# A gated-expert layer behind a long convolution on one core: loop body rotated, set-up reordered

## The chip, the cores and the metric

The kernel runs on one core of one Trainium2 chip. The metric is device time in microseconds (us) of one launch; before the change it is 697.43 us, the median of three runs (694.74 to 697.51).

## The reference, cut to what matters

`x` is 64 sequences x 64 heads x 1024 samples, float32.

```python
# L0, for every head h: a causal convolution over the 1024 samples
mask = (jnp.arange(Lq) < length[:, None])
u_m = u * mask[:, None, :]
kernel = _get_kernel(log_dt, C, log_A_real, A_imag, Lq)   # sum over 64 complex modes of Cs * exp(dtA * l)
y = irfft(rfft(u_m) * rfft(kernel))[..., :Lq] + u_m * D
x = x + y * mask[:, None, :]
# L1, for every (sequence, head) row of 1024
base = x @ W.T
logits = x @ Wr.T + bias_of_language
topw, topi = top_k(logits, 2); weights = softmax(topw)
x = x + base + 2.0 * sum over the two experts of weight * (x @ A_e.T) @ B_e.T
```

## The kernel before

**Pairs.** The work is 32 pairs of heads, numbered i = 0 to 31; a pair has 2 x 64 = 128 rows of 1024 samples. In the code a pair is (b, m) with i = 2b + m, and four heads (two pairs) share one set of generated powers. Every large product is made of three matmuls on float32r halves: high x high, low x high, high x low. ScalarE (ACT) writes the high half (a rounding copy), VectorE (DVE) the low half (the value minus the high half). Names ending in `_hi` and `_lo` are these halves; nearly every one is a hand-off ACT to DVE to TensorE (PE).

**Stages of a pair i.**
- `turn_rows` (PE): eight transposes of the rows of x into the PSUM tile `px`. `split_rows`: ACT copies `px` to `xt` and to `u_hi`, DVE writes `u_lo`.
- `turn_powers` (PE) transposes the generated powers `Z2` into PSUM; `split_ctr` copies them to `c_hi`, `c_lo` and reduces the first 128 samples of the kernel to `k_col`. That column goes to DRAM (`kpad`) and comes back as a Toeplitz tile `toe` (SyncE queue, SP); `split_toe` makes `t_hi`, `t_lo`. `split_obs` makes `zo_hi`, `zo_lo`.
- `control` (PE, 6 matmuls of 448 columns): the input of each block of 128 samples to the modes, into `px` (`v_psum`).
- `scan_states` (DVE, 16 instructions in eight dependent groups of two; ACT swaps real and imaginary halves for it, `copy_states` and three times `swap_odd`): carries the states from block to block. `split_states` makes `s_hi`, `s_lo`.
- `convolve` (PE, 12 matmuls): near part, 6 of 512 columns, from `u` and `t`; far part, 6 of 448 columns, from `s` and `zo`, into `pc`.
- `merge` (DVE) adds it into `xt` where the mask is set; `split_y`: ACT `y_hi`, DVE `y_lo`.
- `project_bank` (PE, 72 matmuls): `y` times the transposed weights in three PSUM banks. The first done (bank 2) holds the router's logits and the experts' 128 inner values. `route` (DVE, 13 small instructions, with one `ratio` from ACT between them) makes `gated`; PE transposes it, `split_gated` halves it, `add_lora` (9 matmuls in all) adds the experts' part. ACT copies the banks to `result` and stores them (`finish`).

**Order.** Each engine has its instructions in an order written by hand; an engine does not pass a waiting instruction. PE's step(b, m), L1132: `convolve(i+1)`, `project_bank(i)` bank 2, `control(i+2)`, `turn_powers(i+3)`, then the other two banks, with the transpose of `gated` and `turn_rows(i+3)` inside the third. DVE's step: `merge(i+1)`, `split_y(i+1)`, `route(i)`, `scan_states(i+2)` with `split_ctr(i+3)`, `split_obs(i+3)`, `split_toe(i+2)` and `split_gated(i)` put between its groups, `split_states(i+2)`, `split_rows(i+3)`. ACT follows the same order. The loop runs 14 times over two steps, and three more steps and a last projection stand behind it.

**Set-up.** The parameters of the modes are computed on DVE in 70 small dependent instructions (`par_step`), among them a polynomial `exact_exp(expo, ...)`. The weights arrive in 11 tiles (`TILE`: A, B, Wr and eight of W), each transposed on PE into a PSUM place, copied to `w_hi` by ACT and to `w_lo` by DVE. The first projection waits (L1042 to L1044 and L1093) until all tiles are done.

Of the kernel before, what the change touches and what calls it, by code (L numbers as in the profile page):

```python
# [13 lines left out]
P = 128  # L14
# [27 lines left out]
def cond_resid_kernel(nc, x, lengths, languages, log_dt, C, log_A_real, A_imag, D, W, Wr, A, B, out):  # L42
    kpad = nc.dram_tensor("kpad", (PAIRS, KPITCH, 2), F32, kind="Internal").ap()
    with ExitStack() as ctx:
# [67 lines left out]


# [38 lines left out]
        xt1_rows = xt[1][:, :, :].rearrange("p c t -> p (c t)")  # L152
        w_rows = [xt1_rows, rows[0][:, :], result[0][:, :], result[1][:, :], result[0][:, :], result[1][:, :],
                  rows[1][:, :], result[1][:, :]]
        a_rows = result[0][:, :]
        b_rows = sb("b_rows", [P, EXPERTS, 8, RANK])
        b_sorted = sb("b_sorted", [P, 8, EXPERTS, RANK])
# [11 lines left out]
        in_pm2 = pm[:, 2, :]  # L169

        def par_psum(k):
# [4 lines left out]
        TILE = [(A_, in_pm, 0), (B_, in_pc, 0), (W_, in_pm, 6), (W_, in_pc, 0), (WR_, in_pm2, 0), (W_, in_pm, 7),  # L176
                (W_, in_pc, 1), (W_, in_pm, 2), (W_, in_pc, 3), (W_, in_pm, 4), (W_, in_pc, 5)]
# [5 lines left out]
        def tile_views(k, wide, narrow):  # L183
            what, place, n = TILE[k]
            if what == B_:
                return place, narrow[:, :].rearrange("e (p o) -> e o p", o=8)
# [32 lines left out]
        sin_ready, z_ready = sem("sin_ready"), sem("z_ready")  # L219
        z_swapped, z2_ready = sem("z_swapped"), sem("z2_ready")  # L220
# [10 lines left out]
        A_STEPS = 25  # L231
        C2_STEPS = 70

        @block.sync
        def _(sp):
# [21 lines left out]
            def load_toe(b, m, first=False):  # L257
                i, s = 2 * b + m, m % 2
                sp.wait_ge(k_stored, 16 * i + 16)
                if not first:  # L260
                    sp.wait_ge(tlo_ready, i - 1)
                sp.dma_start(toe[s][:, :, :], bass.AP(kpad.tensor, i * (2 * KPITCH) + 2, [[2, P], [2, P], [1, 2]])
                             ).then_inc(toe_in[s], 16)

            load_rows(0, 0)
            sp.dma_start(a_rows, A.rearrange("e r d -> (e r) d")).then_inc(a_in, 16)
            sp.dma_start(b_rows[:, :, :, :].rearrange("p e o r -> p e (o r)"),
                         B.rearrange("e (p o) r -> p e (o r)", o=8)).then_inc(b_in, 16)
            sp.dma_start(d_col[:, :], D.rearrange("(h a) -> h a", a=1)).then_inc(d_in, 16)
            for n in (6, 0, 7):  # L270
                load_w(n)
            sp.dma_start(wr_rows[:, :], bass.AP(Wr.tensor, 0, [[P, CH], [LEN, EXPERTS], [1, P]])).then_inc(wr_in, 16)
            sp.wait_ge(px_full, 1)
# [3 lines left out]
            sp.dma_start(len_i[:, :], bass.AP(lengths.tensor, 0, [[0, P], [1, SEQS]])).then_inc(small_in, 16)  # L277
            for h in range(2):
                sp.dma_start(lang_i[h * SEQS:(h + 1) * SEQS, :],
                             languages.rearrange("(b a) -> b a", a=1)).then_inc(small_in, 16)  # L280
            sp.wait_ge(tables, 1)
            sp.dma_start(kpad[:, P:KPITCH, :], zeros[:, :, :]).then_inc(pad_stored, 16)
            sp.wait_ge(pad_stored, 16)
            sp.wait_ge(tables, 3)
            sp.dma_start(bass.AP(kpad.tensor, 2 * P, [[2 * KPITCH, PAIRS], [1, 2]]), k_first[:, :]).then_inc(pad_stored, 16)
            store_kernel(0, 0)
# [3 lines left out]
            load_toe(0, 0, first=True)  # L290
            store_kernel(0, 1)
            load_toe(0, 1, first=True)
            sp.wait_ge(wt_full, w_tile(7) + 1)
            load_w(3)
            sp.wait_ge(wt_full, w_tile(1) + 1)
            load_rows(0, 2)
            sp.wait_ge(wt_full, w_tile(2) + 1)
            load_w(4)
            store_kernel(0, 2)
            load_toe(0, 2)  # L300
            sp.wait_ge(wt_full, w_tile(3) + 1)
            load_w(5)

            def step(b, m, ahead=True):
# [61 lines left out]
        def _(act):  # L366
# [33 lines left out]
            def turn_powers(g, staged, first=False):  # L400

                if not first:
                    act.wait_ge(ct_full, 2 * g)
# [781 lines left out]
```

## Time and profile before

| | |
|---|---|
| runs | 697.51, 697.43, 694.74 us |
| profiled execution, its own time | 695.72 us |
| its span in the profile | 693.9 us |
| PE / DVE / ACT busy | 645.8 / 490.0 / 467.8 us (93% / 71% / 67%) |
| mean granted clock of PE | 0.974 |

What lies around the span is 695.72 - 693.9 = 1.8 us. A row of the timeline gives start, duration, engine, line, operation, output <- inputs, shape; what stands in brackets is how long the engine had been idle and what released it. Two matmuls in a row overlap, so what counts for PE is the distance from start to start.

### The profile page before, as it was taken

Reading aid. Unit: us, or ns where it says so; the run is one execution under the profiler, and the core shown is the slowest. Engines: PE = TensorE matmul, PEld = TensorE weight load, DVE = VectorE, ACT = ScalarE, POOL = GpSimd, SP = SyncE. Lnnn points to the kernel's source line nnn. Section 1 sums busy time; section 2 is a strip of 40 time slices with the busy share of each in tenths; the row PEclk is TensorE's granted clock in tenths of the full one; section 3 lists DMA queues with packets and bytes.
Section 4 is the critical chain, followed back from the end, with each engine's and each line's share of the span. In section 5 each row is a group of like instructions: output and inputs, shape, how many; then the busy total and the mean of one; then the engine's idle time right before and its main releaser. Section 6 shows DMA issues by size and latency. Waiting matters only on the chain.

```text
span 693.9 us, 12598 instructions
## 1 busy us (share of the span) xinstructions
PE 645.8 (93%) x3621; PEld 615.2 (89%) x3621; DVE 490.0 (71%) x1531; ACT 467.8 (67%) x973; POOL 20.4 (3%) x46
## 2 busy tenths in 40 slices
PE   3364999999999999999999999999999999999997
PEld 2353899999999999999999999999999999999997
DVE  8876567777776767777776767777776767777621
ACT  4784577677768677677768677777768677675411
POOL 2000000000000000000000000000000000000000
PEclk9875899999999999999999999999999999999999
DMA  7123023222123233223123233223123223221112
GB/s 241 49 69 89 11 68 70 54 52 68 32 67 68 68 68 68 53 53 68 31 68 68 68 68 68 53 53 68 31 68 68 68 68 68 53 53 39 31 32 60
DMA packets 22869, 43.36 MB, mean 62 GB/s; under 512 B 8104, under 2 KB 13512, under 8 KB 22856
## 3 DMA queue, kind: packets, MB, share of 16 engines
q1 hardware_dynamic: 17576, 26.42, 17.1%
q10 hardware_dynamic: 5280, 16.78, 9.5%
q14 instruction: 7, 0.06, 0.1%
q8 instruction: 6, 0.10, 0.1%
HBM read 26.35 MB, written 16.84 MB: 62 GB/s over the span
## 4 chain that ended last, share of the span: by engine, by line
DVE 36%; ACT 25%; issue 18%; PE 13%; ACTq 6%; DMA 2%; DVEq 1%; SPq 0%
DVE state L783 17%; PE pmg L1104 9%; ACTq L470 5%; ACT result L488 4%; ACT u_hi L416 4%; ACT turn L379 3%; ACT L393 3%; DVE y_lo L830 3%; ACT swapped L439 2%; ACT Z L405 2%; DVE Z L770 2%; ACT xt L413 2%; DVE c_lo L764 2%; ACT z_swap L398 2%; PE pc L1029 2%
## 5 line engine op out<-in xcount | busy, mean ns | idle before, releaser
L1104 PE MATMUL pmg<-w_hi,y_hi 128*128 128x388 f32 (+1 forms) x768 | 268.7, 350 | 1.7 <-ACT result L488 0.2
L1104 PE MATMUL pmg<-w_hi,y_lo 128*128 128x388 f32 (+1 forms) x768 | 260.1, 339 | 0.0
L1104 PE MATMUL pmg<-w_lo,y_hi 128*128 128x388 f32 (+1 forms) x768 | 259.8, 338 | 0.0
L1104 PEld LDWEIGHTS pmg<-w_hi,y_hi 128*128 128x128 f32 x768 | 144.3, 188 | 7.5 <-ACT result L488 6.5
L1104 PEld LDWEIGHTS pmg<-w_hi,y_lo 128*128 128x128 f32 x768 | 144.6, 188 | 0.2
L1104 PEld LDWEIGHTS pmg<-w_lo,y_hi 128*128 128x128 f32 x768 | 144.2, 188 | 0.0
L439 ACT ACTIVATE swapped<-state 64x128 f32<-64x128 f32 x192 | 59.3, 309 | 67.1 <-DVE state L783 65.7
L783 DVE SCALAR_TENSOR_TENSOR state<-swapped,scan_tab,state 128x192 f32<-128x192 f32 (+1 forms) x240 | 73.8, 349 | 12.1 <-ACT swapped L439 0.2
L812 DVE TENSOR_TENSOR s_lo<-state,s_hi 128x896 fp32r<-128x896 f32 x32 | 35.0, 1093 | 31.5 <-ACT s_hi L461 31.5
L744 DVE TENSOR_TENSOR u_lo<-xt,u_hi 128x1024 fp32r<-128x1024 f32 x32 | 39.2, 1225 | 24.8 <-ACT u_hi L416 24.8
L461 ACT ACTIVATE s_hi<-state 128x896 fp32r<-128x896 f32 x32 | 30.5, 953 | 35.0 <-DVE state L783 35.0
L783 DVE SCALAR_TENSOR_TENSOR state<-state,scan_tab 128x64 f32<-128x64 f32 x180 | 50.6, 323 | 0.0
L770 DVE SCALAR_TENSOR_TENSOR Z<-z_swap,gen_tab,Z 128x128 f32<-128x128 f32 x56 | 16.0, 347 | 38.8 <-ACT Z L405 38.8
L824 DVE COPY_PREDICATED xt<-valid,pc 128x512 f32<-128x512 int32 x64 | 42.9, 724 | 0.0
L488 ACT ACTIVATE result<-pmg 128x388 f32<-128x388 f32 (+1 forms) x96 | 37.0, 458 | 8.1 <-PE pmg L1079 7.9
L466 ACT ACTIVATE y_hi<-xt 128x1024 fp32r<-128x1024 f32 x32 | 33.5, 1048 | 13.2 <-DVE xt L824 13.2
L830 DVE TENSOR_TENSOR y_lo<-xt,y_hi 128x1024 fp32r<-128x1024 f32 x32 | 39.0, 1220 | 4.0 <-ACT y_hi L466 3.9
L379 ACT ACTIVATE turn<-pos,phase,gen_tab 128x128 f32<-128x128 f32 x56 | 23.1, 484 | 22.6 <-issue 22.6
L1022 PE MATMUL px<-ident,rows 128*128 128x128 f32 x256 | 35.8, 286 | 0.0
L398 ACT ACTIVATE z_swap<-Z 64x512 f32<-64x512 f32 x32 | 20.2, 630 | 19.5 <-issue 19.0
L1022 PEld LDWEIGHTS px<-ident,rows 128*128 128x128 f32 x256 | 32.1, 149 | 1.2
L413 ACT ACTIVATE xt<-px 128x1024 f32<-128x1024 f32 x31 | 31.3, 1010 | 0.7 <-PE px L1022 0.7
(195 smaller groups left out, 1068.1 us busy)
## 6 DMA issues: line engine op xcount, KB each, us to landing
rows<-in_x SPq DMA_DIRECT2D x64, 256.0 KB, 5.1
out<-result ACTq DMA_DIRECT2D x62, 256.0 KB, 3.0
toe<-kpad SPq DMA_DIRECT2D x32, 128.0 KB, 4.5
result<-in_L_cond_W SPq DMA_DIRECT2D x5, 512.0 KB, 7.2
rows<-in_L_cond_W SPq DMA_DIRECT2D x2, 512.0 KB, 7.8
result<-in_L_cond_A SPq DMA_DIRECT2D x1, 512.0 KB, 5.8
b_rows<-in_L_cond_B SPq DMA_DIRECT2D x1, 512.0 KB, 7.0
xt<-in_L_cond_W SPq DMA_DIRECT2D x1, 512.0 KB, 8.8
```

Source lines behind the costliest of these rows:

```text
L379: ins = nc.scalar.activation(turn[:, h, :], pos[:, :], ACT.Identity, bias=phase[:, 0:1], scale=gen_scalar(TURNS, g, h, staged))
L413: nc.scalar.activation(xt[s][:, :, :], px[:, :, :], ACT.Copy).then_inc(xt_ready, 1)
L439: ins = nc.scalar.activation(swapped[out_half, :, chunks, :], source[in_half, :, chunks, :], ACT.Copy)
L470: act.dma_start(bass.AP(out.tensor, (2 * i + h) * LEN + c0, [[HEADS * LEN, SEQS], [1, c1 - c0]]), result[s][h * SEQS:(h + 1) * SEQS, c0:c1 ...
L488: nc.scalar.activation(result[s][:, c0:c1], pm[:, n, 0:c1 - c0], ACT.Copy).then_inc(pm_free, 1)
L744: vec.tensor_tensor(u_lo[s][:, :, :], xt[s][:, :, :], u_hi[s][:, :, :].bitcast(F32), ALU.subtract).then_inc(ulo_ready, 1)
L783: ins = vec.scalar_tensor_tensor(out=state[:, h, chunks, :], in0=source[:, h, at, :], scalar=scan_scalar(name, m if staged else i, h, staged),
L812: vec.tensor_tensor(s_lo[:, :, :, :], state[:, :, :, :], s_hi[:, :, :, :].bitcast(F32), ALU.subtract).then_inc(slo_ready, 1)
L824: ins = vec.copy_predicated(xt[s][:, :, h * SEQS:(h + 1) * SEQS], valid[:, :, :], pc[:, h, :, :])
L830: vec.tensor_tensor(y_lo[s][:, :, :], xt[s][:, :, :], y_hi[s][:, :, :].bitcast(F32), ALU.subtract).then_inc(ylo_ready, 1)
L1022: ins = nc.tensor.transpose(px[:, c, :], rows[s][:, c * P:(c + 1) * P], ident[:, :])
L1104: ins = nc.tensor.matmul(pm[:, n, 0:c1 - c0], y[s][:, c, :], w[:, c, c0:c1], start=(c == 0 and y is y_hi and w is w_hi), stop=(c == CH - 1 ...
```

## The change

On every engine the step is put in another order. PE: projection of pair i in banks 2 and 0, the transpose of `gated(i)`, `control(i+2)`, `convolve(i+1)`, `add_lora` for two banks, the third bank with `turn_rows(i+3)`. `turn_powers(i+2)` stands at the step's head. So everything is made one pair nearer to its use. DVE: `split_ctr(i+2)`, `split_obs(i+2)`, `route(i)`, `split_rows(i+2)`, `split_toe(i+1)`, `split_gated(i)`, `merge(i+1)`, `split_y(i+1)`, and the scan of pair i+2 with nothing between its groups.

```diff
-            def step(b, m, rows_left=True, ahead=True, kernels=True):
-                convolve(b, m + 1)
-                pe.wait_ge(yhi_ready, 2 * b + m + 1)
-                pe.wait_ge(ylo_ready, 2 * b + m + 1)
-                project_bank(b, m, 0)
+            def step(b, m, rows_left=True, ahead=True):
+                if rows_left:
+                    turn_powers(b, m + 2)
+                wait_y(b, m)
+                project(b, m, 0)
+                project(b, m, 1)
+                turn_gates(b, m, 2 * b + m + 3 if rows_left else PAIRS)
                 if rows_left:
                     control(b, m + 2)
+                convolve(b, m + 1)
+                add_loras(b, m)
+                project(b, m, 2, 0, 7)
                 if ahead:
-                    turn_powers(b, m + 3)
-                project_bank(b, m, 1)
-                project_bank(b, m, 2, ahead)
-
-            with pe.Fori(0, LOOPS) as b:
+                    turn_rows(b, m + 3)
+                project(b, m, 2, 7, 8)
+                add_lora(BANK_ORDER[2])
+
+            with pe.Fori(1, LOOPS) as b:
...
                 for m in range(2):
                     step(b, m)
```

ACT's new step:

```diff
+            def step(b, m, rows_left=True, kernels=True):
+                if rows_left:
+                    split_ctr(b, m + 2)
+                    split_obs(b, m + 2)
+                evacuate(b, m - 1, 2)
+                if rows_left:
+                    split_rows(b, m + 2)
+                ratios(b, m)
+                split_toe(b, m + 1)
                 if kernels and m == 0:
                     act.wait_ge(gen_staged, b + 1)
                     turns_of(None, True)
                 if kernels and m == 1:
                     swap_powers(b + 2)
...
+                store(b, m - 1)
+                split_gated(b, m)
...
                 if kernels and m == 0:
                     magnitudes(None, True)
+                    waves(b + 2)
                 if kernels and m == 1:
...
+                    turn_powers(b + 2, True)
+                for j in range(2):
+                    evacuate(b, m, j)
+                split_y(b, m + 1)
                 if rows_left:
                     copy_states(b, m + 2)
...
+                    for n in range(3):
+                        swap_odd(b, m + 2, n)
+                    if kernels and m == 0:
+                        nc.scalar.activation(warm[:, :], phase[:, 0:1], ACT.Exp)
                     split_states(b, m + 2)
```

The loop runs 13 times (pairs 2 to 27); pairs 0 and 1 are written out ahead of it. `project` is `project_bank` cut into ranges of its eight input chunks; `turn_gates` and `add_loras` are pieces of it.

The set-up:

```diff
-        TILE = [(A_, in_pm, 0), (B_, in_pc, 0), (W_, in_pm, 6), (W_, in_pc, 0), (WR_, in_pm2, 0), (W_, in_pm, 7),
-                (W_, in_pc, 1), (W_, in_pm, 2), (W_, in_pc, 3), (W_, in_pm, 4), (W_, in_pc, 5)]
+        TILE = [(A_, in_pm, 0), (W_, in_pc, 6), (W_, in_pm, 7), (WR_, in_pm2, 0), (W_, in_pm, 0), (W_, in_pc, 1),
+                (W_, in_pm, 2), (W_, in_pc, 3), (W_, in_px, 4), (B_, in_pc, 0), (W_, in_px, 5)]
...
+            def kernel_row(j):
+
+                if j:
+                    pe.wait_ge(k_ready, j)
+                for h in range(2):
+                    ins = nc.tensor.matmul(row_psum[:, j, :], pick[:, h, :], Z2[:, 2 * j + h, :], start=h == 0,
+                                           stop=h == 1, skip_group_check=True)
+                ins.then_inc(row_full, 1)
...
+            def sort_b():
+                act.wait_ge(b_in, 32)
+                nc.scalar.activation(b_sorted[:, :, :, :].rearrange("p o e r -> p e o r"), b_rows[:, :, :, :], ACT.Copy
+                                     ).then_inc(b_ready, 1)
...
+            project(0, 0, 0, 0, 3)
             turn_weight(6)
+            project(0, 0, 0, 3, 6)
+            turn_weight(7)
+            pe.wait_ge(v_copied, 2)
+            pe.wait_ge(scan, SCAN + 1)
+            turn_weight(8)
+            project(0, 0, 0, 6, 8)
+            pe.wait_ge(wlo_ready, w_tile(3) + 1)
+            project(0, 0, 1, 0, 4)
+            turn_weight(9)
+            project(0, 0, 1, 4, 8)
+            turn_weight(10)
+            pe.wait_ge(wlo_ready, 10)
+            convolve(0, 1)
+            turn_gates(0, 0, 2)
```

The first projection starts as soon as the four tiles of bank 2 are split (A, W 6, W 7, Wr). The polynomial for `expo` becomes one ACT exponential (56 parameter steps for 70). The powers of the first four heads are finished in two halves. The first two kernels go to DRAM as rows (`kernel_row`, a matmul with a picking matrix) in place of columns. B is sorted by ACT where GpSimd did it, and loaded in two halves. The loads on SP's queue are reordered to the new order of use; W 0 has a buffer of its own.

On PE, in the loop, the step around the transpose of `gated` (`pc` is the convolution's tile, `px` the control's and the rows', `pmg` the projection's). Before:

```order
L1029 MATMUL pc<-s_lo,zo_hi 128x448
L1029 MATMUL pc<-s_hi,zo_lo 128x448
...
L1104 MATMUL pmg<-w_hi,y_hi 128x384
...
L1029 MATMUL px<-u_hi,c_hi 128x448
L1029 MATMUL px<-u_lo,c_hi 128x448
```

and now:

```order
L1220 MATMUL pmg<-w_hi,y_lo 128x388
L1220 MATMUL pmg<-w_lo,y_hi 128x388
L1229 REGISTER_ALU
L1230 MATMUL pmg<-ident,gated 128x128
L1159 MATMUL px<-u_hi,c_hi 128x448
L1159 MATMUL px<-u_lo,c_hi 128x448
L1159 MATMUL px<-u_hi,c_lo 128x448
L1159 MATMUL px<-u_hi,c_hi 128x448
L1159 MATMUL px<-u_lo,c_hi 128x448
L1159 MATMUL px<-u_hi,c_lo 128x448
L1165 REGISTER_ALU
L1159 MATMUL pc<-u_hi,t_hi 128x512
```

The control of pair i+2 stood 24 projection matmuls behind the convolution of pair i+1; now it stands directly in front of it, and the transpose of `gated(i)` in front of both.

On DVE, in the loop, the rows of the scan and what follows. Before:

```order
L783 SCALAR_TENSOR_TENSOR state<-swapped,scan_tab,state 128x3x64 x2
L762 REGISTER_ALU
L763 TENSOR_REDUCE k_col<-pmg 128x2
L764 TENSOR_TENSOR c_lo<-pmg,c_hi 128x256
L755 SCALAR_TENSOR_TENSOR zo_lo<-Z,sigma,zo_hi 128x256
L796 REGISTER_ALU
L783 SCALAR_TENSOR_TENSOR state<-state,scan_tab 128x64 x2
```

and now, from the scan's last group to the halves that PE waits for:

```order
L885 SCALAR_TENSOR_TENSOR state<-swapped,scan_tab,state 128x3x64 x2
L914 TENSOR_TENSOR s_lo<-state,s_hi 128x896
L855 REGISTER_ALU
L857 TENSOR_REDUCE k_col<-pmg 128x2
L858 TENSOR_TENSOR c_lo<-pmg,c_hi 128x256
L848 SCALAR_TENSOR_TENSOR zo_lo<-Z,sigma,zo_hi 128x256
...
L940 TENSOR_TENSOR logits<-pmg,bias 128x8
...
L964 TENSOR_TENSOR gated<-pmg,gates 128x128
L837 TENSOR_TENSOR u_lo<-xt,u_hi 128x1024
```

`c_lo` and `zo_lo` stood between groups of the scan and now stand behind it; `route` stood in front of the scan and now stands behind it; `u_lo`, which came last, still does, but is now of pair i+2 and not of pair i+3.

## Rows read from the trace of the kernel before

**Rows 1.** The page: busy us, share of the span and instructions of each engine.
```profile
PE 645.8 (93%) x3621; PEld 615.2 (89%) x3621; DVE 490.0 (71%) x1531; ACT 467.8 (67%) x973; POOL 20.4 (3%) x46
```
**Rows 2.** Busy time by stretch: us, PE, PEld, DVE, ACT, POOL, clock, DMA share, GB/s.
```profile
0.00:77.36 77.36, 38.08 (x167) 32.85 (x168) 55.63 (x173) 47.01 (x88) 4.29 (x19) 0.78 0.36 103
77.36:693.90 616.54, 607.74 (x3455) 582.37 (x3453) 434.36 (x1358) 420.76 (x886) 16.07 (x27) 1.00 0.26 57
```
**Rows 3.** Timeline of PE: first matmuls of convolutions 1, 2, 13, 14, 30, and a control.
```profile
74.71 0.47 PE L1029 MATMUL pc<-u_hi,t_hi 128*128 128x512 f32 x1 [0.76 <-DVE w_lo L737]
...
93.88 0.39 PE L1029 MATMUL pc<-u_hi,t_hi 128*128 128x512 f32 x1
...
308.58 0.39 PE L1029 MATMUL pc<-u_hi,t_hi 128*128 128x512 f32 x1
...
315.39 0.36 PE L1029 MATMUL px<-u_hi,c_hi 128*128 128x448 f32 x1
...
316.61 0.38 PE L1073 MATMUL pmg<-ident,Z 128*128 128x128 f32 x2
...
327.72 0.39 PE L1029 MATMUL pc<-u_hi,t_hi 128*128 128x512 f32 x1
...
639.98 0.39 PE L1029 MATMUL pc<-u_hi,t_hi 128*128 128x512 f32 x1
```
**Rows 4.** Timeline of DVE behind the convolution of pair 30.
```profile
642.85 0.15 DVE L816 COPY held<-lang_f 128x1 f32<-128x1 f32 x1 [1.69 <-PE pc L1029]
...
649.90 0.74 DVE L783 SCALAR_TENSOR_TENSOR state<-state,scan_tab,px 128x192 f32<-128x192 f32 x2 [0.57 <-ACT swapped L439]
...
656.69 1.09 DVE L812 TENSOR_TENSOR s_lo<-state,s_hi 128x896 fp32r<-128x896 f32 x1 [1.02 <-ACT s_hi L461]
```
**Rows 5.** Timeline of ACT in the same stretch.
```profile
644.30 1.06 ACT L466 ACTIVATE y_hi<-xt 128x1024 fp32r<-128x1024 f32 x1 [3.43 <-DVE xt L824]
...
648.20 0.60 ACT L447 ACTIVATE state<-px 128x512 f32<-128x512 f32 x1 [0.45 <-PE px L1029]
```
**Rows 6.** Timeline of DVE in the loop: route, c_lo and zo_lo, u_lo, powers.
```profile
316.74 0.16 DVE L838 TENSOR_TENSOR logits<-pmg,bias 128x8 f32<-128x8 f32 x1
...
317.61 0.15 DVE L848 TENSOR_SCALAR half_sum<-ratio 128x1 f32<-128x1 f32 x1
...
319.01 0.74 DVE L783 SCALAR_TENSOR_TENSOR state<-state,scan_tab,px 128x192 f32<-128x192 f32 x2
...
320.45 0.28 DVE L763 TENSOR_REDUCE k_col<-pmg 128x2 f32<-128x128 f32 x1
...
321.38 0.47 DVE L783 SCALAR_TENSOR_TENSOR state<-state,scan_tab 128x64 f32<-128x64 f32 x2
...
328.44 1.23 DVE L744 TENSOR_TENSOR u_lo<-xt,u_hi 128x1024 fp32r<-128x1024 f32 x1 [0.81 <-ACT u_hi L416]
330.49 0.69 DVE L635 TENSOR_TENSOR Z<-angle,mag 128x512 f32<-128x512 f32 x1 [0.81 <-ACT angle L393]
```
**Rows 7.** Timeline of ACT in the loop: s_hi, xt, and the table load.
```profile
325.56 0.95 ACT L461 ACTIVATE s_hi<-state 128x896 fp32r<-128x896 f32 x1 [1.10 <-DVE state L783]
326.42 1.01 ACT L413 ACTIVATE xt<-px 128x1024 f32<-128x1024 f32 x1
...
336.21 1.28 ACT L569 ACT_TABLE_LOAD   x1
337.50 0.20 ACT L569 ACTIVATE warm<-phase 128x1 f32<-128x1 f32 x1
```
**Rows 8.** Timeline of PE in the set-up: first control, and transposes behind idle time.
```profile
23.47 0.71 PE L1029 MATMUL px<-u_hi,c_hi 128*128 128x448 f32 x1 [1.22 <-DVE c_lo L764]
...
64.56 1.94 PE L1002 MATMUL pmg<-ident,result 128*128 128x128 f32 x8 [5.34 <-DVE w_lo L737]
```
**Rows 9.** Timeline of DVE in the set-up: first scan, last low half of a weight tile.
```profile
27.79 0.74 DVE L783 SCALAR_TENSOR_TENSOR state<-state,tab,px 128x192 f32<-128x192 f32 x2 [1.43 <-ACT swapped L439]
...
73.34 1.22 DVE L737 TENSOR_TENSOR w_lo<-pc,w_hi 128x1024 fp32r<-128x1024 f32 x1 [4.10 <-ACT w_hi L370]
```

More of the change, by code:

```diff
@@ L314, in _ @@
                     step(b, m)
-            step(LOOPS, 0)
+            step(LOOPS, 0, rows_left=False)
         @block.gpsimd
@@ new lines, in _ @@
+            split_states(0, 0, first=True)
+            weight(2)
+            split_rows(0, 1, first=True)
+            weight(3)
+            split_obs(0, 1, first=True)
+            split_y(0, 0)
+            weight(4)
+            copy_states(0, 1)
+            weight(5)
+            swap_odd(0, 1, 0)
+            turns_of(1, False)
+            weight(6)
+            swap_odd(0, 1, 1)
+            weight(7)
+            swap_odd(0, 1, 2)
+            waves(1)
+            weight(8)
+            split_toe(0, 1, toe_rows_back)
@@ new lines, in _ @@
+            split_obs(0, 3)
+            evacuate(0, 0, 2)
+            split_rows(0, 3)
+            ratios(0, 1)
+            split_toe(0, 2)
+            act.wait_ge(gen_staged, 1)
+            turns_of(None, True)
+            magnitudes(None, True)
+            store(0, 0)
+            split_gated(0, 1)
+            waves(2)
+            evacuate(0, 1, 0)
+            evacuate(0, 1, 1)
+            split_y(0, 2)
+            copy_states(0, 3)
+            swap_odd(0, 3, 0)
+            swap_powers(2)
@@ L935, in _ @@
-            next(scanning)
+            split_y(0, 1)
+            split_rows(0, 2)
             split_ctr(0, 2)
-            next(scanning)
-            split_toe(0, 1)
-            split_states(0, 1)
             split_obs(0, 2)
-            for k in range(7, WTILES):
-                low_weight(k)
-            split_rows(0, 2)
-            def step(b, m, rows_left=True, ahead=True, kernels=True):
+            dve.wait_ge(scan_staged, 1)
+            for _ in scan_states(0, 2):
+                pass
@@ new lines, in _, with step @@
+            split_states(0, 2)
+            split_ctr(0, 3)
+            split_obs(0, 3)
+            route(0, 1)
+            split_rows(0, 3)
+            split_toe(0, 2)
+            angles(2)
+            split_gated(0, 1)
+            merge(0, 2)
+            powers(2)
+            split_y(0, 2)
+            for _ in scan_states(0, 3):
+                pass
+            rotate_powers(2, True)
+            split_states(0, 3)
+            def step(b, m, rows_left=True, kernels=True):
+                if rows_left:
+                    split_ctr(b, m + 2)
+                    split_obs(b, m + 2)
@@ L1158, in _ @@
[L1158 to L1162 removed]
+            step(LOOPS, 0)
+            step(LOOPS, 1, ahead=False)
+            step(LOOPS + 1, 0, rows_left=False, ahead=False)
+            wait_y(LOOPS + 1, 1)
+            project(LOOPS + 1, 1, 0)
+            project(LOOPS + 1, 1, 1)
+            turn_gates(LOOPS + 1, 1, PAIRS)
```

574 lines of the change are left out of this document (314 added, 260 removed).

## Prediction

> **What bounds the kernel now.** I read the page first: PE is busy 93% of the span, DVE 71%, ACT 67% [rows 1]. Split by stretch it falls into two kernels [rows 2]. Up to 77.4 us, where the first projection starts, PE is busy 38.1 of 77.4 us at a granted clock of 0.78: a set-up bound by chains. From there PE is busy 607.7 of 616.5 us at clock 1.00: PE is the bound, and DVE (434.4) and ACT (420.8) have some 180 us of room by their sums. The timeline of PE gives the beat. From the convolution of pair 2 (93.88) to that of pair 30 (639.98) there are 28 intervals: 546.1 / 28 = 19.50 us a pair [rows 3]. Between those of pairs 13 and 14, where PE never waits, it is 327.72 - 308.58 = 19.14 us; that is PE's own work for a pair. So the loop can give 0.36 us x 28 = 10 us at most, and the set-up more. What the shares do not tell is how long the chain through DVE and ACT is from one convolution to the next, and the change lengthens just that.
>
> **The loop: the chain that the new order makes.** Let N be the start of a convolution's first matmul, pair i. I follow DVE's new program from there, with durations of the old trace.
>
> 1. `held` starts at N + 2.87 (639.98 to 642.85), `y_hi` at N + 4.32 (644.30) [rows 3 to 5]. In the new order `copy_states(i+1)` stands directly behind `y_hi`: 1.06 less the 0.09 by which two ACT instructions overlap, then 1.70 to the scan's first instruction (648.20 to 649.90) [rows 4, 5]. The scan starts at N + 6.99.
> 2. From there to `s_lo` the row has 6.79 us (649.90 to 656.69) [rows 4], with `t_lo` and `gt_lo` (0.54 together) standing in holes where DVE waits for ACT's swaps. Without them the holes remain: I take 6.64. `s_lo` starts at N + 13.63. In every other step (m = 0) ACT loads the exponential's table and runs `warm` between the last swap and `s_hi`: 1.29 + 0.20 [rows 7], of which 1.06 lie beside the scan's last group. Behind such a step `s_lo` starts 0.43 later, at N + 14.06.
> 3. `s_lo` 1.00 start to start, then `k_col`, `c_lo`, `zo_lo` 0.93 (320.45 to 321.38) [rows 6]: N + 15.56, or N + 15.99. In steps m = 1 `powers` comes in between, 0.69 less 0.09 of overlap [rows 6]: 16.59.
> 4. `route`: 0.87 to `half_sum`, which needs ACT's `ratio`. `s_hi` starts 0.98 before `s_lo` (its 0.95 and a hand-off), and on ACT follow `s_hi` 0.86, `c_hi` 0.28, `zo_hi` 0.40, a bank's copy 0.40, `xt` 0.90, `u_hi` 0.95 (start to start, as s_hi and xt in [rows 7]) and `ratio` 0.29: N + 16.73 in steps m = 0. So `half_sum` starts at N + 16.76 (m = 0) and at 16.59 + 0.87 = N + 17.46 (m = 1).
> 5. From `half_sum` to the next instruction 1.40 (317.61 to 319.01), then `u_lo` 1.23 [rows 6]: done at N + 19.39 or N + 20.09. The control of pair i+2 can start some 0.12 later (a first matmul behind `c_lo` in [rows 8] came 0.15 after it) and takes 316.61 - 315.39 = 1.22 [rows 3]. Then the next convolution starts: **N + 20.72 or N + 21.42**, mean 21.07.
>
> PE by itself would be there at N + 19.14. In the old order the control's half `u_lo` was made a pair ahead, the far part alone waited for `s_lo`, and `c_lo`, `zo_lo` lay in the holes of the scan. Now `s_lo`, `c_lo`, `route` and `u_lo` stand one behind the other, and control and the whole convolution (3.8 us of PE) stand behind their end. The price is 21.07 - 19.50 = 1.57 us a pair. Nothing hides it: PE's other 15 us of the pair are issued ahead of the wait and lie beside the chain already. ACT has no wait of its own in it: `gt_hi`, the waves and the two bank copies end just before `y_hi` is due (by my count with 0.1 us of room in steps m = 0, so it can only add). SP's loads of rows and Toeplitz tiles are issued a whole pair ahead of use, as before, and cost nothing.
>
> **The set-up.** 14 parameter steps go, and the rest is better placed: parameters 1.7 us earlier. With the first powers in two halves the first control starts at about 20.1 for 23.47 [rows 8]. ACT then has weight tiles and the second half to do, so the first scan starts at 26.2 for 27.79 [rows 9]; convolution 0 ends at 37.3, `y_lo` of pair 0 at 41.2. The first projection starts at 42.6 for 77.4, cut up by the transposes of the last tiles, which still come at the rate of ACT and DVE: the last low half is done at 62.6 for 73.34 + 1.22 = 74.6 [rows 9]. The third bank ends at 69.2; `y_hi`, `xt`, `u_hi` of the next two pairs stand in line on ACT (3 x 1.0 us), control 2 starts at 73.6, the projection of pair 1 at 75.0, its two banks are done at 84.7. Then comes the chain of steps 2 to 5 for the first time: scan at 76.6, `route(1)` ends at 87.9, `t_lo(2)` at 89.4. Convolution 2 starts at **89.6** for 93.88 [rows 3], 4.3 us earlier, and PE has by then done two banks of pair 1 besides, 8.5 us of matmuls that the old order did later. So the set-up alone is worth 4.3 + 8.5 = 12.8 us. The transposes in it run at half rate behind idle time (1.94 us for eight at 64.56, [rows 8]); where PE now stays busy they are shorter, which is in the figures. The row form of the first two kernels (four 128-column matmuls, two small copies), ACT's sort of B (about 1.0 us) and the small extra loads lie beside other work: if the sort were bare, it would cost 1 us once.
>
> **The sum.** Convolution 2 at 89.6. Step 2 is irregular: ACT has the swap and the scaling of the next heads' powers between its three swaps of the state (2.5 us, less 0.2), so convolution 3 starts 23.0 later, 112.6. Then 13 steps of 21.42 and 12 of 20.72 (pairs 3 to 27): 527.1, to 639.7. Two steps without kernels, 20.72 each: 681.2. The last convolution comes 17.35 later, there is no control in front of it: 698.5. Behind it on PE three banks, two banks, and the rest, 22.6, last copy 0.5, last store 3.7: span 725.4. With 1.8 around it 727.2 us against 695.7 of the profiled execution: 31.5 us or 4.5% slower. The profiled execution lies 1.7 below the median of 697.4; I forecast **728 us**.
>
> Between bounds: the chain cannot be under PE's 19.14 a pair, and the sum of its parts with each of about twelve hand-offs 0.05 us shorter or longer gives 20.5 to 21.7 a pair, 16 us down and 18 up over 28 pairs.
>
> **A rule against the trace.** The table load in the chain lasts 1.28 us, and `warm` starts 0.01 us behind it [rows 7]. The Trainium skill (ScalarE: Activation LUTs, What ACT_TABLE_LOAD costs) gives a switch of tables as about 2.66 us, with a drain behind the load. By that figure every other step would be 1.38 us longer, 13 x 1.38 = 18 us in all, an estimate of 745 us. The row shows no such drain, so the sum goes by the row.
>
> **The rivals.**
> - *The chain is hidden* (10%). If waits overlap better than I count and the beat stays PE's own, the gain of the set-up stands: 695.7 - 12.8 = 682.9, and with 0.2 to 0.3 us a pair of the old waits gone too some 676; say 682. For it: DVE is busy only 14.3 of 19.5 us a pair. Against it: an in-order queue adds its waits, and the old trace shows them (1.02 before `s_lo`, 0.81 before `u_lo`, [rows 4, 6]). The point from which it decides is a beat under 21.07 - 31.5 / 28 = 19.95 us.
> - *A draw* (5%): a beat of 19.8 to 20.1, 692 to 700 us.
> - *ACT late too* (7%). The 0.1 us of room in steps m = 0 is gone as soon as ACT's two stores or register work cost more than I count. Each us there comes back on `y_hi` and delays everything: 13 us a microsecond; 742 us.
> - *The table's drain* (3%), 745 us, as above.
> - *The clock falls in the waits* (2%). PE will stand idle 1.6 to 2.3 us in each pair. In the old trace matmuls behind 5.3 us of idle ran at half rate [rows 8], at clock 1.2 GHz for 2.4; gaps of this length after full rate it does not show. If control and convolution ran at 1.2 GHz, 3.8 us more would stand in the chain each time: over 100 us. The Trainium skill (TensorE: Matmul & The Clock Gate, HAM oscillation) warns of loops in which every round's wait brings the slow clock back.
> - *The change doesn't do what it says*: if the first projection had to wait for the last tile all the same, the set-up would give only 2 or 3 us and the whole came to 738. It is in the range.
>
> My forecast has the remaining 73%.
>
> **How the numbers follow.** Range: 20 us below 728 (a beat of 20.35, a little beyond the lower bound of the hand-offs, because I may have counted waits twice) and 14 above (a beat of 21.55, or ACT late by a microsecond): 708 to 742. That leaves out the hidden chain, the draw and the far tail, some 2 in 10. Faster by over 0.5% (about what a measurement can tell from no change): the 10% of the hidden chain and a part of the draw, 0.11. Within 0.5%: 0.04. Slower: 0.85.
>
> **What would show it.** In the new profile: convolutions 20.7 and 21.4 us apart by turns; PE busy some 88 to 90% of the span at clock 1.00 in the loop; a wait of PE at the control's matmul for DVE's `u_lo`, or at the transpose of `gated`, of 1.6 to 2.3 us a pair and some 50 us in all; `ratio` holding DVE 0.3 us in steps m = 0; convolution 2 at about 90 us. Wrong would be: a beat of 19.2 with PE's waits near nothing; PE released by ACT's bank copies or by SP's loads; or a first projection not before 60 us.

## The result, and the profile after

The changed kernel takes 735.30 us (median of 4 runs, 733.52 to 736.74) against 696.36 us of the kernel before in the same session (4 runs, 694.74 to 697.51): a ratio of 1.056, 95% interval 1.052 to 1.060. The forecast was 728 us, in a range of 708 to 742. The profiled execution took 734.07 us, its span 732.3.

Page of the changed kernel, busy time of the engines (the same lines of before are [rows 1]):

```profile
PE 658.6 (90%) x3629; PEld 616.8 (84%) x3629; DVE 495.0 (68%) x1518; ACT 465.5 (64%) x980; POOL 19.1 (3%) x38
```

Its work by stretches (columns: stretch, length, busy time and instructions of PE, weight loads, DVE, ACT and POOL, PE's granted clock, DMA share, GB/s):

```profile
0.00:42.00 42.00, 24.27 (x100) 19.69 (x101) 34.26 (x125) 27.49 (x55) 1.07 (x9) 0.80 0.54 161
42.00:96.00 54.00, 42.66 (x237) 39.33 (x235) 34.92 (x94) 34.98 (x70) 0.40 (x2) 0.91 0.23 54
96.00:679.00 583.00, 543.93 (x3033) 512.04 (x3032) 403.50 (x1223) 386.69 (x821) 17.65 (x27) 0.99 0.24 54
679.00:732.30 53.30, 47.71 (x264) 45.76 (x263) 22.36 (x78) 16.36 (x35) 0.00 (x0) 0.99 0.18 43
```

Before, PE had waited 8.8 us in all the 616.5 behind the set-up [rows 2]. Now it is idle 39 of 583 us in the third stretch, at a clock of 0.99. The first projection begins at 42.5 us for 77.4; the forecast was 42.6.

PE's waits in the loop, 115 to 690 us (waiting instruction, its releaser, us in total, times, longest):

```profile
PE px L1152 <- DVE state L885: 11.4, 27, 0.5
PE px L1159 <- DVE u_lo L837: 10.1, 13, 0.8
PE px L1159 <- issue: 8.2, 14, 0.6
PE pmg L1230 <- DVE gated L964: 5.6, 13, 0.4
```

PE ahead of the convolutions 14 and 15 (start, us, engine, line, operation, tiles; idle time before it):

```profile
349.68 0.32 PE L1230 MATMUL pmg<-ident,gated 128*128 128x128 f32 x1 [0.44 <-DVE gated L964]
350.78 0.44 PE L1159 MATMUL px<-u_hi,c_hi 128*128 128x448 f32 x1 [0.78 <-DVE u_lo L837]
...
352.09 0.40 PE L1159 MATMUL pc<-u_hi,t_hi 128*128 128x512 f32 x1
...
371.38 0.44 PE L1159 MATMUL px<-u_hi,c_hi 128*128 128x448 f32 x1 [0.58 <-issue]
...
372.66 0.39 PE L1159 MATMUL pc<-u_hi,t_hi 128*128 128x512 f32 x1
```

And DVE between these two convolutions:

```profile
354.98 0.15 DVE L918 COPY held<-lang_f 128x1 f32<-128x1 f32 x1 [3.76 <-PE pc L1159]
...
359.06 0.74 DVE L885 SCALAR_TENSOR_TENSOR state<-state,scan_tab,px 128x192 f32<-128x192 f32 x2 [0.32 <-ACT swapped L479]
...
365.61 1.09 DVE L914 TENSOR_TENSOR s_lo<-state,s_hi 128x896 fp32r<-128x896 f32 x1 [1.02 <-ACT s_hi L501]
...
368.67 0.15 DVE L950 TENSOR_SCALAR half_sum<-ratio 128x1 f32<-128x1 f32 x1 [0.17 <-ACT ratio L510]
...
370.06 1.22 DVE L837 TENSOR_TENSOR u_lo<-xt,u_hi 128x1024 fp32r<-128x1024 f32 x1
```

N is, as in the forecast, the start of a convolution's first matmul, here 352.09. This is the chain of the forecast. `u_lo` ends at 371.28, the control's first matmul starts 0.10 later ("issue" is that wait, whose releaser the record lacks), and the convolution stands behind it. In the steps between convolutions 3 and 28 the intervals are 20.57 us (steps m = 0, to an odd convolution) and 21.42 us (steps m = 1, to an even one) by turns, mean 525.5 / 25 = 21.02 us (before: 19.50).

The waits are smaller than the forecast's sign for them, which was 1.6 to 2.3 us a pair at the control or the transpose of `gated`, some 50 us in all. They are 0.44 + 0.78 = 1.22 us in steps m = 1 and 0.58 in steps m = 0, 23.9 us in all; another 11.4 us stand earlier in the step, at the transposes of the rows (L1152), until the scan has read its input out of `px`.

One place was not foreseen. In the loop's first step PE stands at the transposes of the next heads' powers, which now head the step:

```profile
108.37 0.69 PE L1201 MATMUL pmg<-ident,Z 128*128 128x128 f32 x2 [4.40 <-DVE Z L864]
108.71 0.67 PE L1220 MATMUL pmg<-w_hi,y_hi 128*128 128x384 f32 x1
109.18 0.52 PE L1220 MATMUL pmg<-w_hi,y_lo 128*128 128x384 f32 x1
...
113.26 0.34 PE L1220 MATMUL pmg<-w_lo,y_hi 128*128 128x384 f32 x1
```

DVE rotates these powers only behind the scan of pair 3. PE waits 4.4 us, and then multiplies at the lower clock: 15 matmuls start 0.32 us apart for 0.18, until 113, which is 2.1 us. Behind that it waits for nothing up to the convolution. From convolution 2 (91.06) to 3 (120.61) it takes 29.55 us; the forecast had 23.0. The wait and the slow matmuls together, 4.4 + 2.1 us, are as much as the 6.5 between them.

### The profile page after: what moved, and what is told of

It reads as the page before. It is cut to its first block, busy times and chain, and to the rows that moved or that the text cites. A ratio compares the mean times of both kernels' runs of the same rounds, so it can differ in the third digit from the quotient of the medians.

```text
span 732.3 us, 12371 instructions
## 1 busy us (share of the span) xinstructions
PE 658.6 (90%) x3629; PEld 616.8 (84%) x3629; DVE 495.0 (68%) x1518; ACT 465.5 (64%) x980; POOL 19.1 (3%) x38
## 4 chain that ended last, share of the span: by engine, by line
PE 44%; DVE 24%; ACT 16%; issue 14%; ACTq 0%; DVEq 0%; DMA 0%; SPq 0%
PE pmg L1220 22%; PE pc L1159 12%; ACT swapped L479 7%; DVE state L885 6%; PE px L1159 6%; DVE xt L926 5%; DVE u_lo L837 3%; ACT state L487 3%; PE px L1152 2%; ACT s_hi L501 2%; ACT L668 2%; PE pmg L1207 1%; DVE held L918 1%; DVE zo_lo L848 1%; DVE c_lo L858 1%
## 5 line engine op out<-in xcount | busy, mean ns | idle before, releaser
L524 ACT ACTIVATE result<-pmg 128x388 f32<-128x388 f32 (+1 forms) x96 | 43.4, 453 | 100.7 <-PE pmg L1207 100.2
L918 DVE COPY held<-lang_f 128x1 f32<-128x1 f32 x96 | 14.8, 154 | 101.1 <-PE pc L1159 98.9
L932 DVE TENSOR_TENSOR y_lo<-xt,y_hi 128x1024 fp32r<-128x1024 f32 x32 | 39.2, 1225 | 24.0 <-ACT y_hi L506 22.5
L1159 PE MATMUL px<-u_hi,c_hi 128*128 128x448 f32 x64 | 26.3, 410 | 23.7 <-DVE u_lo L837 10.1
L1152 PE MATMUL px<-ident,rows 128*128 128x128 f32 x256 | 35.9, 285 | 11.4 <-DVE state L885 11.4
L1152 PEld LDWEIGHTS px<-ident,rows 128*128 128x128 f32 x256 | 28.8, 145 | 20.2 <-DVE state L885 19.2
L1159 PEld LDWEIGHTS px<-u_hi,c_hi 128*128 128x128 f32 x64 | 12.2, 191 | 31.0 <-issue 30.5
L837 DVE TENSOR_TENSOR u_lo<-xt,u_hi 128x1024 fp32r<-128x1024 f32 x31 | 37.7, 1215 | 0.7 <-ACT u_hi L456 0.7
L456 ACT ACTIVATE u_hi<-px 128x1024 fp32r<-128x1024 f32 x31 | 32.0, 1031 | 0.0
```

What stands on the lines that cost most here:

```text
L524: nc.scalar.activation(result[s][:, c0:c1], pm[:, n, 0:c1 - c0], ACT.Copy).then_inc(pm_free, 1)
L837: vec.tensor_tensor(u_lo[s][:, :, :], source[:, :, :], u_hi[s][:, :, :].bitcast(F32), ALU.subtract).then_inc(ulo_ready, 1)
L932: vec.tensor_tensor(y_lo[s][:, :, :], xt[s][:, :, :], y_hi[s][:, :, :].bitcast(F32), ALU.subtract).then_inc(ylo_ready, 1)
L1152: ins = nc.tensor.transpose(px[:, c, :], rows[s][:, c * P:(c + 1) * P], ident[:, :])
L1159: ins = nc.tensor.matmul(out, l, r, start=first and n == 0, stop=last and n == 2, skip_group_check=True)
```

## Experiments

Unless said otherwise each is the changed kernel with one edit. Ratios are to the kernel before on the same chip. A beat is the interval between the first matmuls of two convolutions in a row; the longer one is that of steps m = 1, the shorter one that of steps m = 0. The runs are numbered in the order in which they were made.

**1. More PE work: does PE or the chain set the beat?**

```diff
+                if j == 1 and c0 == 0:
+                    for _ in range(6):
+                        nc.tensor.matmul(pm[:, n, 0:o1 - o0], y_hi[s][:, 0, :], w_hi[:, 0, o0:o1], start=True,
+                                         stop=False, skip_group_check=True)
```

> The changed kernel with six more matmuls of 388 columns a pair (repeats of the first one, each overwriting the last) ahead of bank 0, 6 x 0.177 = 1.06 us of PE work in front of the place where PE waits. If the chain through DVE sets the beat (my theory), the wait takes it up: in its trace PE waits 1.2 us in steps m = 1 and 0.6 us in steps m = 0 there, so 0.0 and 0.5 us a pair remain, some 5 to 9 us in all: 741 to 744. If PE sets the beat (rival), 31 x 1.06 = 33 us more: 768.

740.84 us, 1.0636 (1.0619 to 1.0654). Some 33 us of matmuls cost 5.5. The longer beat stays (21.46 for 21.42), the shorter one grows by 0.27 (20.84), since 1.06 us are more than the 0.58 that PE waited there, and it now waits there no more. In the changed kernel PE's work lies beside the chain; it is not the bound.

**2. More DVE work in the chain.** A second subtraction of half the size, 0.54 us start to start, in front of `s_lo`:

```diff
+                vec.tensor_tensor(spare[:, :, :], state[:, 0, :, :], s_hi[:, 0, :, :].bitcast(F32), ALU.subtract)
```

> The changed kernel with one more DVE subtraction of 448 elements a pair into an unused tile, directly in front of s_lo; 0.5 to 0.6 us. If the chain sets the beat, nothing absorbs it: 30 x 0.55 = 16 us more, 751 to 753. If DVE's idle time (32% of the span) is room (rival), no change: 735.

765.45 us, 1.0999 (1.0981 to 1.1018): 30 us more, twice what the chain explains. Where the convolutions keep their rate, the beats are 22.09 and 20.87, together 0.97 more than before the edit, about the 0.54 twice, less the 0.17 of `ratio`'s wait, now covered. Over 13 rounds that is 13 us. The rest came out only with run 6: in 11 steps matmuls of the convolution last up to 0.63 us in place of 0.39, and such a pair of steps is 1.5 to 1.6 us longer. In some of them the control is slow already:

```profile
273.25 0.59 PE L1161 MATMUL px<-u_hi,c_hi 128*128 128x448 f32 x1 [0.78 <-DVE u_lo L838]
```

**3. The control behind the convolution and the two `add_lora`.**

```diff
-                if rows_left:
-                    control(b, m + 2)
                 convolve(b, m + 1)
                 add_loras(b, m)
+                if rows_left:
+                    control(b, m + 2)
```

> The changed kernel's steady step with control(i+2) behind convolve(i+1) and its two banks' add_lora, all other orders as they are. Chain theory: the convolution then waits for t_lo, which ends 0.3 us behind u_lo, and not for u_lo and the control's 1.22 us; the beat falls by 0.9 us, 28 x 0.9 = 25 us: 710, beats of 19.7 and 20.5. Rival (the control's place is harmless, the time sits in the late s_lo or in route alone): 730 to 735.

715.11 us, 1.0270 (1.0253 to 1.0287): 20 us less, where I had expected 25. The beats are 20.70 and 19.85. The convolution does not wait for `u_lo` any more but for `t_lo`, which stands right behind it on DVE (1.27 and 0.48 us by turns). So the gain is smaller than with the whole chain gone: `route` and `u_lo`, which stand in front of `t_lo` on DVE, still hold the convolution.

**4. The transposes of the powers behind the first bank, in every step.**

```diff
-                if rows_left:
-                    turn_powers(b, m + 2)
                 wait_y(b, m)
                 project(b, m, 0)
+                if rows_left:
+                    turn_powers(b, m + 2)
```

> The changed kernel's steady step with turn_powers(i+2) behind the first bank and not in front of it. The trace of the changed kernel has one wait of 4.40 us of PE at turn_powers in step 2, for the powers that DVE rotates behind the scan; this wait stood in none of my terms. If it is what my sum of the start lacked, it goes and the first steps are 4 to 8 us shorter, once: 728 to 731, steady beat as it is. Rival: the late powers hold the step anyway through c_lo: 735.

747.20 us, 1.0737 (1.0719 to 1.0755), 12 us more where I had expected less. The first step did shrink (24.0 us for 29.55), but the loop's beats became 21.58 and 21.58. ACT shows why:

```profile
409.84 0.95 ACT L501 ACTIVATE s_hi<-state 128x896 fp32r<-128x896 f32 x1 [1.02 <-DVE state L885]
411.68 0.39 ACT L475 ACTIVATE c_hi<-pmg 128x256 fp32r<-128x256 f32 x1 [0.89 <-PE pmg L1201]
```

`c_hi` reads what these transposes write; they come 0.9 us late for it, and `xt`, `u_hi`, `ratio` stand behind it in the queue. At the step's head they are early in the loop and late only once.

**5. The kernel before, with the control alone moved in front of the convolution.**

```diff
             def step(b, m, rows_left=True, ahead=True, kernels=True):
+                if rows_left:
+                    control(b, m + 2)
                 convolve(b, m + 1)
...
                 project_bank(b, m, 0)
-                if rows_left:
-                    control(b, m + 2)
```

> The kernel BEFORE, with one edit in the loop's steps: the control of pair i+2 stands in front of the convolution of pair i+1, the place it has in the changed kernel; what feeds it stays where it was, so its low half u_lo is made a pair ahead. My theory (the price is the chain c_lo, route, u_lo that the new order puts in front of the control, not the control's place): c_lo is there some 4 us before the control was issued in the old order, but only about when the convolution starts, so PE waits a little at most; beat 19.5 to 19.8 a pair, 696 to 704 us. Rival (the place alone, control and its copies in the chain, costs its own 1.2 us each pair): 28 x 1.2 = 34 us, about 730.

774.91 us, 1.1129 (1.1092 to 1.1166): far outside both expectations. My reading of the old order was wrong. In this run PE's control waits for `u_lo`:

```profile
409.24 1.23 DVE L744 TENSOR_TENSOR u_lo<-xt,u_hi 128x1024 fp32r<-128x1024 f32 x1 [0.80 <-ACT u_hi L416]
```

```profile
410.56 0.44 PE L1029 MATMUL px<-u_hi,c_hi 128*128 128x448 f32 x1 [1.93 <-issue]
```

`u_lo` was not made "a pair ahead". In the kernel before it is the last work of DVE's preceding step: for pair 15 it ends at 329.67 us (328.44 + 1.23, [rows 6]), 1.95 behind the start of convolution 14. The control came only at 334.91, behind that convolution and a bank:

```profile
334.91 0.36 PE L1029 MATMUL px<-u_hi,c_hi 128*128 128x448 f32 x1
```

These 5.2 us were the cover, and moving the control in front of the convolution takes them away: the beats at full rate are 21.4 to 21.8. In 13 of the loop's steps the convolution ran at half rate besides. So the control's place is no harmless part of the change; alone it costs more (79 us) than with DVE's program turned to suit it (39 us).

**6. The table load and `warm` behind `s_hi`.**

```diff
-                    if kernels and m == 0:
-                        nc.scalar.activation(warm[:, :], phase[:, 0:1], ACT.Exp)
                     split_states(b, m + 2)
+                    if kernels and m == 0:
+                        nc.scalar.activation(warm[:, :], phase[:, 0:1], ACT.Exp)
```

> The changed kernel with the loop's table load and warm (once in two steps) behind split_states in place of in front of it. My theory: s_hi no longer waits for the load, s_lo of steps m = 1 starts 0.43 us earlier, but the load then stands between s_hi and c_hi, so that c_hi, xt, u_hi and ratio of that step still come late. DVE's side (s_lo, c_lo, route) is a product of px and pc and waits for ACT only at ratio and u_lo: at best 13 x 0.43 = 5.6 us less, 729.7; if ratio holds DVE instead, no change (735). Rival (the drain of the table switch of 2.66 us is hidden somewhere in the chain): 13 x 1.3 = 17 us less, 718.

752.95 us (750.0 to 758.0), 1.0799 (1.0755 to 1.0843). `s_lo` did start earlier, but the load now stands in front of `c_hi`, and `c_lo` needs that; I had overlooked it:

```profile
353.35 1.09 DVE L914 TENSOR_TENSOR s_lo<-state,s_hi 128x896 fp32r<-128x896 f32 x1 [1.02 <-ACT s_hi L501]
355.14 0.29 DVE L857 TENSOR_REDUCE k_col<-pmg 128x2 f32<-128x128 f32 x1 [0.69 <-ACT c_hi L475]
...
357.93 0.15 DVE L950 TENSOR_SCALAR half_sum<-ratio 128x1 f32<-128x1 f32 x1 [0.17 <-ACT ratio L510]
```

That makes one step of two 22.12 us for 21.42: 9 us in 13 steps. It is not the 17.6 measured. The rest is on PE; the rows are of the slowest of the four executions (758.0):

```profile
402.23 0.33 PE L1230 MATMUL pmg<-ident,gated 128*128 128x128 f32 x1 [1.10 <-DVE gated L964]
403.33 0.44 PE L1159 MATMUL px<-u_hi,c_hi 128*128 128x448 f32 x1 [0.78 <-DVE u_lo L837]
...
404.63 0.53 PE L1159 MATMUL pc<-u_hi,t_hi 128*128 128x512 f32 x1
404.96 0.63 PE L1159 MATMUL pc<-u_lo,t_hi 128*128 128x512 f32 x1
```

The six matmuls of the control still run at full rate. Then those of the convolution, 0.39 to 0.40 us each in the changed kernel, take 0.63. (This is one step; in others of this run the control is slow as well.) The granted clock of the stretch from 96 to 300 us is 0.95, against 0.98 there in the changed kernel. This happened in 9 of the steps (the expectation of run 9 says 10), always in those with the longer waits, and costs 1.5 us each time: 9 + 9 x 1.5 = 22.5 us, which is this execution's excess (758.0 - 735.3 = 22.7). The median has 17.6; how many slow steps the other executions had is not on record.

**9. The same kernel with PE's wait filled.** Five matmuls into a free bank, in front of the transpose of `gated`, in steps m = 1:

```diff
+                if rows_left and m == 1:
+                    pe.wait_ge(pm_free, 3 * (2 * b + m) + 3)
+                    n = BANK_ORDER[2]
+                    o0, o1 = BANKS[n]
+                    for _ in range(5):
+                        nc.tensor.matmul(pm[:, n, 0:o1 - o0], y_hi[1][:, 0, :], w_hi[:, 0, o0:o1], start=True,
+                                         stop=False, skip_group_check=True)
                 turn_gates(b, m, 2 * b + m + 3 if rows_left else PAIRS)
```

> The kernel with warm behind s_hi (753 us), and in its steps m = 1 five extra matmuls (0.9 us, into the third bank's region, which its first matmul overwrites) right in front of the transpose of gated, where PE stood idle 1.1 us. They do nothing but fill the wait. In that kernel the convolutions behind the longer waits (1.1 + 0.78 us) ran at half rate in 10 of 28 steps (512 columns in 0.63 us instead of 0.39), and with a step's 0.7 us of real delay (c_hi behind the table load, 13 times, 9 us) this should make up its 17.6 us over the changed kernel. My theory (the idle time of PE ahead of the convolution, not the delay, brings the half rate): with the fill all convolutions run at full rate, beats 22.1 and 20.6 all through, 743 to 746 us, 8 to 10 less for 12 us more of PE work. Rival (the half rate comes from elsewhere, or the extra matmuls stand in the chain): 753 or more.

743.13 us (742.97 to 744.04), 1.0662 (1.0644 to 1.0680): as expected, 9.8 us less for more work. At the corresponding place:

```profile
395.18 1.04 PE L1327 MATMUL pmg<-w_hi,y_hi 128*128 128x388 f32 x5
396.45 0.32 PE L1230 MATMUL pmg<-ident,gated 128*128 128x128 f32 x1 [0.22 <-DVE gated L964]
397.55 0.45 PE L1159 MATMUL px<-u_hi,c_hi 128*128 128x448 f32 x1 [0.78 <-DVE u_lo L837]
...
398.87 0.40 PE L1159 MATMUL pc<-u_hi,t_hi 128*128 128x512 f32 x1
```

`gated` and `u_lo` come as late as before; only PE's idle time is gone, and every convolution of the loop runs at full rate. The beats are 22.11 and 20.57 throughout. So the half rate goes when the idle time is filled, and the delay of 0.7 us in 13 steps remains: 743.1 - 735.3 = 7.8, by the spans 741.2 - 732.3 = 8.9.

**7. The convolution in front.** On PE `convolve(i+1)` stands ahead of the turned gates and the control. `t_lo` heads the steps of DVE, `t_hi` those of ACT, and ACT's waves, magnitudes and scaled powers stand in front of `gt_hi`:

```diff
+                convolve(b, m + 1)
                 turn_gates(b, m, 2 * b + m + 3 if rows_left else PAIRS)
                 if rows_left:
                     control(b, m + 2)
-                convolve(b, m + 1)
                 add_loras(b, m)
```

and on DVE and ACT

```diff
             def step(b, m, rows_left=True, kernels=True):
+                split_toe(b, m + 1)
                 if rows_left:
...
-                split_toe(b, m + 1)
```

> The changed kernel with the convolution of pair i+1 in front of the turned gates and the control of pair i+2, as in the kernel before; on DVE and ACT t_lo and the magnitudes, waves and scaled powers stand at the head of their steps so that nothing of the convolution waits for the control. The new set-up and everything else stay. My theory (the chain through u_lo to the convolution is the whole loss, the set-up is a gain of about 10 us): the beat returns to PE's own 19.2 to 19.5, so 28 x (21.02 - 19.35) = 47 us less than the changed kernel: 682 to 690 us, faster than both. Rival (the loss lies in the rotation as such, stores, loads and copies of banks in other places): a beat of 20.5 or more, 715 to 735.

696.81 us (10 runs), 1.0002 (0.9985 to 1.0020). The chain is out of the way: beats 19.52, 38.5 us less than the changed kernel. But that is no faster than the kernel before, where I had expected 682 to 690. The set-up's gain has gone into the first steps: convolution 2 starts at 93.07 us, and convolution 4 starts 47.64 later, where the kernel before has 38.59 between them (93.88 to 132.47). In the loop's first step the wait for the rotated powers stands here too, 4.39 us.

**8. The same, with the transposes of the powers late as in run 4.** What is moved is PE's `turn_powers`, not ACT's scaling of the powers, which the expectation names.

> As the run before, and ACT's scaling of the next powers behind the first bank's copy of PE's program rather than ahead of it. In the first steps the scaling of powers held PE 4.4 us at the changed kernel's convolution 3, and moving it late took 5.5 us from that step and gave it back at c_hi in each later one. With the convolution first, c_hi is not in the chain that sets PE's beat: I expect the 4 to 5 us of the start and no loss later, so 4 us below the run before. Rival (c_hi still binds): 5 to 10 us above it.

698.01 us, 1.0030 (1.0009 to 1.0051). From convolution 2 to 4 it is 40.99 us, 6.6 less. Every other beat of the loop is 20.04 in place of 19.52 and gives that back: `half_sum` waits up to 0.8 us for `ratio`, which stands behind `c_hi`.

**10. The first step apart.** In the changed kernel, PE's first two steps are written out, and only the first has the transposes late:

```diff
+            step(1, 0, late=True)
+            step(1, 1)
-            with pe.Fori(1, LOOPS) as b:
+            with pe.Fori(2, LOOPS) as b:
```

> The changed kernel with PE's first two steps written out ahead of its loop (the loop begins one round later, the other engines' programs stay) and, in the very first of them alone, the transposes of the next powers behind the first bank in place of in front of it. That is the step in which PE waited 4.4 us for DVE's rotated powers and lost 6.5 us against my prediction. With the transposes late in every step it got shorter by 5.5 us and all others longer by 0.6. My theory (a start-up order alone costs the 6.5): 5 to 6 us less than the changed kernel, 729 to 730, beats as there. Rival (another wait behind it, for c_hi or the state, takes its place): 735.

731.01 us, 1.0488 (1.0468 to 1.0508), 4.3 us less. Convolution 3 comes 24.97 us behind convolution 2 for 29.55; the beats stay 20.57 and 21.44. Most of the unforeseen term is this order in one step. In it PE now waits at the end of the chain (0.5 us for `gated`, 0.9 for `u_lo`); the 1.9 us that are left of the 6.5 stay open.

**11. The same with the convolution in front.**

> The kernel with the convolution in front (696.8 us, beats 19.52), and the same two steps written out. There the steps from convolution 2 to 4 took 47.6 us, with the late transposes 41.0. Expected: 6 to 7 us less, 690 to 691 us, 0.8% faster than the kernel before. Rival (the following steps give it back): 697.

694.12 us (692.24 to 694.42, 6 runs), 0.9949 (0.9934 to 0.9964). Only 2.7 of the 6 to 7 us: the step to convolution 3 is 21.85 for 28.12, but the next one 23.11 for 19.52, with PE waiting 2.2 us for `gt_lo` there. About 4 us of start-up stay open.

**12. As 11, and the rows of pair i+3 turned behind the last chunk.**

```diff
-                if ahead:
-                    turn_rows(b, m + 3)
                 project(b, m, 2, 7, 8)
+                if ahead:
+                    turn_rows(b, m + 3)
```

> As the run before, and the transposes of the rows of pair i+3 behind the third bank's last matmuls in place of before them. In the loop of the kernel with the convolution in front PE's only wait is at these transposes, for DVE's last read of the state's v in px (some 0.5 us a pair). Expected: a beat of 19.1 to 19.3 for 19.52, 6 to 10 us less than the run before, 681 to 685 us. Rival (xt and u_hi, which read the turned rows, are then late for the next control): no gain, 690.

684.39 us (681.79 to 686.63, 6 runs), 0.9808 (0.9784 to 0.9832): 1.9% faster than the kernel before, 6.9% faster than the changed one. Between 115 and 660 us PE's only wait in run 7 was this (25 times; the weight loads of these transposes waited up to 0.5 us for the same):

```profile
PE px L1152 <- DVE state L885: 4.1, 25, 0.2
```

In run 12 it is gone; from 125 us on PE is never idle:

```profile
125.00:650.00 525.00, 525.00 (x3003) 506.21 (x3002) 396.93 (x1208) 371.17 (x797) 4.91 (x25) 1.00 0.27 59
```

The beats are 19.14 and 19.36. The first is what the kernel before took where PE never waited, [rows 3]; both are now PE's own work for a pair.

## Why the prediction was right, and where it was not

**The bound** (view of PE's beat, [rows 3]): right. The chain that the new order closes through `s_lo`, `c_lo`, `route`, `u_lo` and the control sets the beat: run 1 shows that PE does not, run 3 that a good part of the loss goes with the control out of the convolution's way (a mean beat of 20.27 us for 21.02), run 7, which changes the order on three engines at once, that all of the loop's loss goes with `route` and `u_lo` out of it too (19.52).

**The chain's steps.** In a step m = 0: `held` at N + 2.89 for 2.87, the scan at N + 6.97 for 6.99, `s_lo` at N + 13.52 for 13.63, `half_sum` held 0.17 for 0.3, `u_lo` to control 0.10 for 0.12. The beats are 20.57 and 21.42 for 20.72 and 21.42, over pairs 3 to 28 525.5 us for 527.1. The scan took 6.55 us to `s_lo` where I had left 6.64 for its holes. The beat of 21.42 is right to the hundredth by luck: in steps m = 1 `s_lo` started 0.14 earlier than forecast (344.55 - 330.63 = N + 13.92 for 14.06), and the control took 1.31 us up to the convolution for the 1.22 in the sum. The sign for PE's waits was twice too large (23.9 us for 50): I had put the whole difference to PE's 19.14 into one wait, but 11.4 us of it stand at the transposes of the rows, and the rest is no idle time in the view.

**The set-up:** the first projection at 42.5 us for 42.6 was right, and convolution 2 at 91.06 for 89.6 was 1.5 late. The step to convolution 3 is **the term that was mis-sized**: 29.55 us for 23.0. I had counted ACT's work between its swaps there, but not that DVE rotates the powers behind the scan while PE's transposes of them stand in front of all else, nor that PE then multiplies at the lower clock. The wait of 4.4 us and 2.1 us of slow matmuls are as much as the term lacked, and run 10 took back 4.6 us of the 6.5. The account from 725.4 to the span of 732.3: + 1.5 + 6.5 - 1.6 in the loop, + 0.5 in the last steps and the end (27.4 us behind the last convolution for 26.9).

**The gain of 12.8 us** ascribed to the set-up was there only in part. Run 7, whose beat equals that of before, ends level with it: 0.8 us at convolution 2, 7.4 at the end (28.5 us behind the last convolution's start for 35.9), and 9.1 lost in the two steps between. The 8.5 us of matmuls done early do show at the end, as 7.4, but the two first steps lose more than that. Why the start-up costs so much is in part shown (the 4.4 us wait) and in part open (some 4 us, run 11).

**The old cover.** The sentence that `u_lo` was made a pair ahead was wrong; it had 5.2 us of room, given by the convolution and a bank in front of the control (run 5). The sum did not rest on it.

**The rivals.** ACT late: not seen in the loop, where `y_hi` starts at N + 4.33 in both kinds of step (356.42 and 376.99 us) for the 4.32 of the forecast. The chain hidden, and the draw: excluded by the beat. The table's drain: `warm` starts 0.01 us behind the load in the changed kernel too (342.18 + 1.28, then 343.47), and beats of 21.42 leave no place for it. Of the 2.66 us that the Trainium skill (ScalarE: Activation LUTs, What ACT_TABLE_LOAD costs) gives for a switch, this kernel pays the load alone. The clock in the waits, which I gave 2%: not in the changed kernel's loop, whose waits before a convolution are 0.44 + 0.78 us or 0.58. But it was near. With 0.96 + 0.78, 1.10 + 0.78 and 2.0 us of idle time (runs 2, 6, 5) it did come, in 11, 9 and 13 steps, at 1.2 to 1.6 us each, not 3.8.

## What to carry to other kernels

An operation that only the pair after next needs must stand behind the one that the next pair waits for. Putting it in front tied a whole pair's chain of copies to the next convolution here, even while DVE and ACT had room by their sums. When a kernel is turned like this, draw the chain from one beat to the next through the in-order queues with the old trace's durations; that came within 0.1 us a pair here. Treat the first round of the loop apart, and look for the cover of each moved operation: what ended late there unnoticed.

## What was not expected of the hardware

PE fell to half rate behind waits of 1.7 to 2.0 us in a step otherwise full of matmuls (granted clock 0.80 from 400 to 408 us in run 6). It did so in some steps and not in others with the same waits. Run 6 scattered with it (750.0 to 758.0 us, and 742.97 to 744.04 with the wait filled), runs 2 and 5 did not (2.5 and 1.2 us between the fastest and the slowest). Where the fall begins varies: at the convolution in the step shown of run 6 (404.63), at the control's first matmul in that of run 2 (273.25). Filling the wait with matmuls that do nothing saved 9.8 us. The Trainium skill (TensorE: Matmul & The Clock Gate, HAM oscillation) tells of this for waits that are longer than the matmuls between them; here the waits were less than a tenth of the step.
